# Deformable convolution on one core: strips sampled in six units of tap row and column half, instead of two column halves

## The reference, cut to what matters

```python
om = conv3x3_same(align, om_w, om_b)            # per position: 8 groups x 9 taps x (dy, dx, mask)
off, mask = om[..., :144], sigmoid(om[..., 144:])
for each of the 8 channel groups (32 channels) and the 9 taps:
    val = bilinear(coarse_up, own place + tap + off) * mask    # 0 outside the image
out = einsum('bhwkc,kcf->bhwf', val, weight) + bias            # 9 x 256 channels -> 256
return relu(out) + fine_cal
```

## Time and profile before

| | |
|---|---|
| median of 3 runs | 3745.19 us |
| the profiled execution's own time | 3750.21 us |
| its span, first to last instruction | 3748.5 us |
| TensorE busy | 3383.5 us, 90% |
| VectorE busy | 2643.4 us, 71% |
| ScalarE busy | 1636.7 us, 44% |
| GpSimd busy | 1300.2 us, 35% |
| mean granted TensorE clock | 0.956 |
| `sample_and_project` | from about 1376 us to the end |

### The profile page before, as it was taken

One profiled execution on the slowest core, in us unless ns is written; L12 is line 12 of the kernel. 1 busy time (PEld: TensorE's weight loads), 2 busy tenths in 40 slices (PEclk: granted clock), 3 DMA queues, 4 the chain that ended last, 5 costly groups with the idle time before them and its releaser, 6 DMA issues.

```text
span 3748.5 us, 103646 instructions
## 1 busy us (share of the span) xinstructions
PE 3383.5 (90%) x39276; PEld 3082.7 (82%) x39276; DVE 2643.4 (71%) x4029; ACT 1636.7 (44%) x3018; POOL 1300.2 (35%) x1358
## 2 busy tenths in 40 slices
PE   8979999999999947998888998998899898988998
PEld 7869999999999936888787887887788787877888
DVE  3446666666666548878876887886887887688882
ACT  0021211211221215656654665664666665566663
POOL 1000000000000025645645555554654655455451
PEclk9989999999999978999998999998999998999998
DMA  4232232222223221111112111112111112111110
GB/s 160 78 122 42 48 72 42 48 53 39 51 51 43 32 49 30 29 32 31 31 32 32 32 33 29 31 34 32 29 33 31 30 34 36 25 33 32 31 27 23
DMA packets 352248, 159.43 MB, mean 43 GB/s; under 512 B 228724, under 2 KB 346884, under 8 KB 351620
## 3 DMA queue, kind: packets, MB, share of 16 engines
q1 hardware_dynamic: 325456, 109.56, 17.4%
q10 hardware_dynamic: 21724, 26.37, 2.1%
q0 software_dynamic: 4608, 16.78, 1.2%
HBM read 104.60 MB, written 55.23 MB: 43 GB/s over the span
## 4 chain that ended last, share of the span: by engine, by line
PE 44%; issue 7%; ACT 6%; DVE 2%; POOL 2%; ACTq 1%; DMA 1%; SPq 1%; POOLq 0%; DVEq 0%
PE eb L1420 25%; PE tb L981 9%; PE vb L1003 9%; ACT wtT L986 4%; ACT ot L1025 1%; ACT res L1012 1%; DVE wt L975 1%; PE tb L911 1%; DMA win<-cpad 1%; ACTq L1316 1%; PE vb L1018 1%; ACT val L1289 1%; ACTq L882 0%; DVE val L1362 0%; SPq L1083 0%
## 5 line engine op out<-in xcount | busy, mean ns | idle before, releaser
L1420 PE MATMUL eb<-val,wd 128*128 128x256 f32 (+2 forms) x8172 | 1269.5, 300 | 9.5 <-POOL gate L1212 8.5
L1420 PEld LDWEIGHTS eb<-val,wd 128*128 128x128 f32 x8172 | 1080.6, 199 | 44.8 <-issue 35.4
L975 DVE TENSOR_TENSOR wt<-taps_all 128x576 f32<-128x576 f32 x1024 | 938.6, 984 | 52.5 <-PE tb L981 44.6
L981 PE MATMUL tb<-ident,wt 128*128 128x128 f32 x4608 | 715.9, 282 | 63.8 <-ACT wtT L986 45.3
L986 ACT COPY wtT<-tb 128x512 f32<-128x512 f32 x1152 | 651.8, 593 | 164.8 <-PE tb L981 126.0
L1362 DVE TENSOR_TENSOR val<-vb,val 128x432 fp32r<-128x432 f32 (+1 forms) x768 | 382.6, 552 | 411.0 <-ACT val L1289 409.2
L981 PEld LDWEIGHTS tb<-ident,wt 128*128 128x128 f32 x4608 | 504.7, 141 | 185.5 <-ACT wtT L986 103.6
L1289 ACT CAST val<-vb 128x432 fp32r<-128x432 f32 (+1 forms) x768 | 342.1, 524 | 706.4 <-PE vb L1003 706.2
L480 PE MATMUL conv<-fine,wf 128*108 128x256 f32 x4608 | 591.1, 289 | 7.6 <-DVE omT L751 7.6
L480 PEld LDWEIGHTS conv<-fine,wf 128*108 128x108 f32 x4608 | 570.5, 173 | 23.0 <-issue 23.0
L1003 PE MATMUL vb<-wtT,win 64*32 64x144 f32 x16384 | 350.2, 309 | 184.3 <-issue 93.3
(11 more groups left out here) (138 smaller groups left out, 3175.7 us busy)
## 6 DMA issues: line engine op xcount, KB each, us to landing
win<-cpad SPq DMA_DIRECT2D x304, 64.0 KB
om_s<-om_d SPq DMA_DIRECT2D x1152, 12.0 KB
chunk<-in_x SPq DMA_DIRECT2D x32, 512.0 KB, 5.9
xchunk<-in_x SPq DMA_DIRECT2D x32, 512.0 KB, 4.2
r_d<-r POOLq DMA_DIRECT2D x32, 512.0 KB, 3.2
rt<-r_d SPq DMA_DIRECT2D x63, 256.0 KB, 2.9
out<-ot ACTq DMA_DIRECT2D x63, 256.0 KB, 2.2
om_d<-omT SPq DMA_DIRECT2D x64, 216.0 KB
```

Of the source, the lines that this page charges most:

```text
L975: return nc.vector.tensor_tensor(wt[:, g * NK:(g + 1) * NK, WQ * u:WQ * (u + 1)].rearrange("p k (a b) -> p k a b", a=WIN), of_group(0).uns ...
L981: last = nc.tensor.transpose(tb[b][:, 128 * j:128 * j + 128], wt[:, 4 * i + j, :], ident[:])
L1420: done = nc.tensor.matmul(eb[fo][:, W * r0:W * r1], wd[wp][:, half, k, 128 * fo:128 * fo + 128], source[:, at:at + r1 - r0, cols], start=f ...
```

## The change

**Units.** A strip is sampled in six units, `UNITS` = 6: three tap rows `d` (in the order of `ROWS` = 2, 1, 0) times two column halves. Unit `at` has `d` = at // 2 and `hx` = at % 2. `wt` and `wtT` keep their size, and hold three units (`n_sub`), each with 3 taps x 4 groups for both channel halves. One sampling matmul (`sample`) has 3 taps x 16 positions = 48 moving columns, and there are 8 x 2 x 4 = 64 in a unit, 384 in a strip, where 128 with 144 columns were. A unit's values fill two banks (`vb[b]`, one for each channel half), in two buffers. ScalarE casts both halves in one operation of 768 elements (`keep_values`), VectorE splits in two of 384. The outer products are 12 for a strip, 128 x 768 elements each (`tap_weights_of`).

**Rows and banks.** `val` has 10 rows: even parity in 2 to 5, odd in 6 to 9, rows 0 and 1 are copies of 8 and 9. So no projection matmul is in two pieces any more. The copies are made by SyncE's queue, `duplicate_rows`, once in two strips: 4 DMAs, each 128 partitions x 6 taps x one run of 2 x 66 floats (528 bytes), after the sides of the odd strip. `open_strip` of the even strip waits for them (`duplicated`). The exchange at an image's end needs no `held`. A strip projects into one bank of its own, `eb[q]`, the output halves side by side; `turn_result` writes into the same bank, and one copy of 512 elements takes it out.

**Positions** are made on VectorE (`locate`, 10 steps and `coef`), where GpSimd had `place` and `weigh`. `cap` is in two parts, in two slots.

**The order.** A slot is one unit. TensorE has in each: batch 0, 5 projection matmuls, the sampling of the unit before, batch 1, 7 projection matmuls, batch 2, 6 projection matmuls; the projection is three units behind. Windows are loaded in 8 DMAs of 32 KB, near half and far half each when their last unit is sampled.

The core of the diff (`general`, constants and the setup left out):

```diff
-        VROWS, VCOLS = 9, W + 2
+        VROWS, VCOLS = 10, W + 2
-        vb = [[bank(f"vb{u}{i}") for i in range(2)] for u in range(2)]
+        vb = [ctx.enter_context(nc.psum_tensor(f"vb{i}", [128, CH, 512], f32)) for i in range(2)]
...
+        def sample(sub, b, window):
+            for j in range(BLK):
                 for u in range(2):
-                    for g in range(GH):
+                    for c in range(GH):
                         part = slice(WQ * u, WQ * (u + 1))
-                        weights = wtT[part, g * NK:(g + 1) * NK].rearrange("p k (y x) -> p k y x", y=4)
-                        last = nc.tensor.matmul(bank_of(u, v)[32 * g:32 * g + 32, :, :, at:at + 4],
-                                                win[part, window(j), 32 * g:32 * g + 32], weights[:, :, :, 4 * j:4 * j + 4],
+                        weights = wtT[part, PER * sub:PER * (sub + 1)].rearrange("p (k c) (y x) -> p c k y x", k=3, y=4)
+                        last = nc.tensor.matmul(values_of(b)[32 * c:32 * c + 32, u, :, :, 4 * j:4 * j + 4],
+                                                win[part, window(j), 32 * c:32 * c + 32], weights[:, c, :, :, 4 * j:4 * j + 4],
                                                 start=True, stop=True)
...
+                def duplicate_rows(s):
+                    w(sp, "sides", done)
+                    w(sp, "projected", read)      # 3 * (s - 1)
+                    for v in val:
+                        for half in range(CH):
+                            sp.dma_start(v[:, half, 0:6, 0:2].bitcast(f32), v[:, half, 0:6, 8:10].bitcast(f32)
+                                         ).then_inc(sems["duplicated"], 16)
...
+            # GpSimd
+                        for at in range(UNITS):
+                            side(*unit(t, p, at, -1))
+                            if at == 0:
+                                measure(t + 1, 1 - p, 0)
+                            if at == 1:
+                                measure(t + 1, 1 - p, 1)
+                            if at == 2:
+                                open_strip(t, p, crossing if p == 0 else None)
+                            if at == TURN_AT:
+                                add_rest(t - 1)
...
+            # ScalarE
+                def slot(t, p, at):
+                    for i in range(3):
+                        if known(t, 0, ST):
+                            w(act, "batched", batch_no(t, at, i) + 1)
+                            copy_batch("act", n_sub(at), i, bank_no(t, p, at, i)).then_inc(sems["tb_out"], 1)
+                        if i == 0:
+                            keep_values(*unit(t, p, at, -1))
+                    if at == 0:
+                        taps(t + 1, 1 - p, 0)
+                    if at == OM_AT and known(t + 2, 0, ST):
+                        keep(t + 2, batch_no(t, OM_AT, 3), bank_no(t, p, OM_AT, 3))
+                    if at == 2:
+                        taps(t + 1, 1 - p, 1)
...
+            # VectorE
+                def slot(t, p, at):
+                    products(*unit(t, p, at, 2))
+                    split_values(*unit(t, p, at, -1))
+                    if at in (1, 3):
+                        begin_cap(t + 1, 1 - p, at // 2)
+                    if at in (2, 4):
+                        end_cap(t + 1, 1 - p, at // 2 - 1)
+                    if at == 5:
+                        locate(t + 2, p)
...
+            # TensorE; OM_AT, FINISH_AT, TURN_AT, RESULT_AT = 1, 3, 4, 5
+                def project_part(s, p, d, half, piece):
+                    if known(s, 0, ST + 1):
+                        if half == 0 and piece == 0:
+                            w(pe, "ready", s + 1)
+                            if d == 0:
+                                w(pe, "ob_out", s - 1)
+                            elif known(s, 0, ST):
+                                w(pe, "sides", UNITS * s + 2 * d + 2)
+                        last = project(s, p, d, range(EACH * half + AFTER[piece], EACH * half + AFTER[piece + 1]))
+                def slot(t, p, at):
+                    target, q, pos = unit(t, p, at, -3)
+                    for i in range(3):
+                        if known(t, 0, ST):
+                            if i == 0:
+                                w(pe, "products", 2 * (n + 1))
+                            w(pe, "tb_out", batch_no(t, at, i) - 1)
+                            transpose_batch(n_sub(at), i, bank_no(t, p, at, i)).then_inc(sems["batched"], 1)
+                        project_part(target, q, pos // 2, pos % 2, i)
+                        if i == 0:
+                            sample_unit(*unit(t, p, at, -1))
+                    if at == OM_AT and known(t + 2, 0, ST):
+                        offsets_turn(t + 2, batch_no(t, OM_AT, 3), bank_no(t, p, OM_AT, 3))
+                    if at == TURN_AT and known(t - 1, 0, ST + 1):
+                        w(pe, "summed", t)
+                        turn_result(1 - p, m).then_inc(sems["turned"], 1)
```

More of the change, by code:

```diff
@@ L1048, in known, with unit @@
                 return not isinstance(v, int) or least <= v < end
+            def unit(t, p, at, ahead):
+                n = at + ahead
+                more, pos = n // UNITS, n % UNITS
+                return t + more, (p + more) % 2, pos
             def loop(e, strips):
@@ L1122, in sp_fast @@
                     load_offsets(sp, s, True, sems["om_loaded"])
-                strip(0, 0, None)
-                for i in range(1, 4):
-                    strip(0, i, i)
-                with sp.Fori(1, 4) as m:
-                    for i in range(4):
-                        strip(0, 4 * m + i, i)
+                batch(0)
                 with sp.Fori(1, B - 1) as b:
@@ L1257, in pool_fast @@
                     strips(it)
-                for it in range(8 * B - 1, 8 * B + 2):
+                for it in range(8 * B - 1, 8 * B + 1):
                     strips(it)
@@ L1413, in project @@
                         source = val[vp][:, half, k]
[L1414 to L1421 removed]
+                        first, last = d == 0 and n == 0, d == 2 and n == len(todo[d]) - 1
+                        at = dy + 4 * q
+                        done = nc.tensor.matmul(eb[q][:, 256 * fo:256 * fo + rows], wd[wp][:, half, k, 128 * fo:128 * fo + 128],
+                                                source[:, at:at + rows // W, cols], start=first, stop=last)
                     return done
@@ L1578, in dve_general @@
[L1578 to L1584 removed]
+                                        dst = sums[u][hx][:, 3 * ROWS[d]:3 * ROWS[d] + 3]
```

614 lines of the change are left out of this document (279 added, 335 removed).

## The result

The changed kernel took 4179.73 us (median of 4 runs, 4173.78 to 4195.98), the kernel before 3744.85 us (4 runs): a ratio of 1.117, 95% interval 1.113 to 1.121. It is 435 us slower, where 3910 us was forecast. The profiled execution took 4173.78 us with a span of 4172.1.

What follows compares the result with a forecast made beforehand. TensorE was taken as the bound: a strip of 30.6 us work plus 6.75 of waits is +2.35, times 64 +150; with +15 for image starts on 3750.2, less 5, 3910 us. Range 3650 to 4110.

Steps and rivals of the forecast that it cites:

- The sign: Whole kernel: slower 0.71, faster 0.24, same 0.05.
- Sampling's pace: TensorE's sampling bursts: 0.0085 us a matmul, 8.2 us a strip, +2.7 over the kernel before.
- The order's waits: TensorE waits for work GpSimd lists behind `side`: 2.4 (`measure`, slot 1), 0.8 (`ready`, slot 2), 1.85 us (`add_rest`, slot 4).
- The gate: `ready` on GpSimd, slot 2: done at 5.5 us against 5.4; with VectorE's `cap`, a wait of 0.8 us (0.1 to 1.5).
- The cast: ScalarE's cast of a unit's samples: begins 2.77 us into a slot and takes 0.8 us.
- in every second strip the 3.11 us of the loop's turn lie there instead. Together 1.7: Slot 1's first projection matmuls wait for side columns, or TensorE's loop turns there: 1.7 us a strip (1.55 to 3.4).
- Some 3.9 us are waits: Kernel before, per strip: beside 29.6 us of TensorE work and 1.55 of loop turn, some 3.9 us are waits.
- The pieces: Projection matmuls no longer cut in two: -1.8 us a strip on TensorE, all on the path.
- VectorE: Takes the positions at 3.6 us; busy 31.3 us a strip, not the bound, but little is spare.
- Duplicates: DMA row copies taken as hidden in some 12 us; rival, chance 0.10: late, about 4070, or 4325 at 25 us.
- An image's start: Window loads have less time before TensorE wants them: +5 us each, three times, +15.
- Sampling stays bound by issue: Rival, chance 0.07: sampling matmuls stay at 0.0172 us each, +6.7 us a strip, about 4340 us.

Runs made afterwards that it cites:

- e13_changed_unrolled: Changed kernel with `measure` and `add_rest` moved ahead of `side` and middle column's projection first (3879 us), TensorE's loop unrolled by seven pairs of strips: 3869 us, ratio 1.032.
- e4_before_ten_rows: The kernel before with only the changed kernel's ten-row layout of values, shared rows copied by DMA: 3665 us, ratio 0.978.
- e7_after_wide: Changed kernel with one sampling matmul of 96 columns for two of 48 (values wrong, only time of use): 3976 us, ratio 1.062.
- e9_first_and_wide: Changed kernel with `measure` and `add_rest` ahead of `side`, and 96-column sampling matmuls (values wrong): 3683 us, ratio 0.983.

## Why the prediction was wrong

The sign (slower, with a chance of 0.71) and the order of the waits on other engines were right; 3910 us was 270 too low, and the range ended at 4110. Two steps failed: the price of fetching instructions, and the 3.9 us of the kernel before that were taken for waits. TensorE's waits in the ten strips of the kernel before (all but one of 0.3 us), then the three kinds of issue gap in those of the changed kernel:

```profile
PE vb L1003 <- issue: 16.6, 5, 3.5
PE vb L1003 <- ACT wtT L986: 8.2, 5, 1.6
...
PE tb L981 <- ACT wtT L986: 5.6, 10, 0.6
...
PE tb L911 <- ACT wtT L986: 2.1, 11, 0.2
```

```profile
PE vb L1012 <- issue: 18.1, 14, 1.8
...
PE tb L993 <- issue: 15.4, 10, 2.0
...
PE eb L1462 <- issue: 2.9, 5, 0.8
```

- **Sampling's pace** was right. Forecast 128 matmuls in 1.37 us with the way in and out of the burst (0.0085 each and 0.28); a clean burst takes 1.31, a clean slot 5.01 for 4.95. The 25 ns between starts of the Trainium skill ("TensorE: Matmul & The Clock Gate", section "Wait — 56ns, not 53.3ns?"), already doubted then, do not hold for this tiling: the starts are 10.2 ns apart on average.
- **The order's waits**, 2.4, 0.8 and 1.85 us a strip, 5.05 in all: 323 us. The runs that moved `measure` and `add_rest` gave 248, with the side columns 301. In the trace the addition costs 1.57 a strip (ten strips), the copy 1.28 as a mean and 2.42 where it shows in full. The gate costs 1.54 and is the mis-sized one. Only a part of that is the side column (0.78 us for 0.49). The cast was even a little early (it begins 2.60 us into the slot for 2.77); what was late was VectorE. The forecast gave it 2.3 us of `cap` ahead of slot 2, but did not carry the late distances of slot 0 on to it.
- **"in every second strip the 3.11 us of the loop's turn lie there instead. Together 1.7"** is the step that failed. I took the one gap of the kernel before and carried it over, as a price of the jump. The changed kernel has three times the sampling instructions, and fetching them was priced at nothing more. The trace has 3.64 us of issue a strip (18.1 + 15.4 + 2.9 over ten) and 0.39 for the side columns, 4.03 for 1.7: some 149 us over 64 strips. `e13_changed_unrolled` and the packets show that these gaps are no price of the jump. All waits that the trace counts come to 8.4 us a strip for the 6.75 forecast.
- **"Some 3.9 us are waits"** failed too, and as much hangs on it. These 3.9 us are what the sum of the kernel before left over beside the loop's turn. The trace of its ten strips shows only 1.6 us a strip of such waits, and 1.7 for the turn. The other 2.1 to 2.3 us were neither work in the sum nor a wait, and the forecast dropped them when it put the new waits in by name. They are still there: work was forecast at 30.6 us a strip, and 41.88 less 8.4 leaves 33.5, 2.9 more. At 2.1 us over 64 strips that is some 134 of the 270 us.
- **The clock** is a part of that rest and was no term of the sum. By the granted clock of the ten strips, 0.96 for 0.98, it costs at most 1.7 us a strip now and 0.7 before, an estimate (0.04 x 41.88, 0.02 x 34.98). A strip of the kernel before at clock 1.00 (31.70 us) has a rest of 1.5 us with no clock in it: 27.8 by the prediction's sum without the pieces, 2.4 of waits. A part is that a gap's printed idle time is shorter than the loss from start to start, since ends are modelled. What the rest is beyond that stays open.
- **The pieces**: 1.8 us a strip was the price, and alone they gave 1.2 net (`e4_before_ten_rows`).
- **VectorE**: 28.4 us a strip for 31.3, the positions 3.1 us (2556.33 to 2559.38) for 3.6. Not the bound, as said. What I did not ask is whether moving them brings anything: it brought nothing, twice.
- **Duplicates** hidden, as forecast; that rival is out. **An image's start** was forecast 5 us dearer and is some 4 cheaper.
- **A reading**: 48 sampling matmuls "end at 2547.38" in the prediction. In the trace the last of them starts at 2547.26 and ends at 2547.55. Nothing hangs on it.
- **"Sampling stays bound by issue"** (4340, chance 0.07) came nearest among the rivals in kind, not in number (late duplicates at 4070 are nearer to 4180), and by the wrong mechanism. It priced a slower pace within a burst; what happens is that bursts at full pace run out of instructions.

The account by runs, all from medians: before 3745; ten rows of values -80; the chain through GpSimd +301; pace and fetching of narrow sampling matmuls +249 (with the order set right). Sum 4215, measured 4180. The 35 us between were not taken apart. A wait and a gap can cover each other in the changed kernel, as `e7_after_wide` and `e9_first_and_wide` show (204 us with the waits in place, 249 without), and the starts of the images are cheaper.

## What to carry to other kernels

Cutting an operation in pieces of equal work has a price per instruction that no instruction's duration shows: beside the pace, count how many instructions a stage issues per microsecond, and look at where the profile puts idle time down to issue, whether that comes at the loop's turn or in the middle of a burst, and whether it ends a fixed time after a packet of the instruction queue has landed. When stages are made shorter, a fixed chain through three engines no longer fits behind one; in a list worked in order, put first what another engine waits for (three calls moved here: 248 us). When a sum of work and waits leaves something over, do not call it waits before the trace shows them: it may come back under the new order. And try the parts of a large change alone: the ten rows of values with TensorE's loop unrolled make a kernel of 3548 us, 5.3% faster than the one before and 15% faster than the whole change.

## What the hardware showed that was not expected

- Matmuls of 48 columns on a 64x32 piece of the array start 10.2 ns apart on average in a burst, of 72 columns 11.4 ns, of 144 columns 17.2 ns.
- Instructions run dry within one burst: after 242 and after 116 matmuls (each with its weight load), for 2.17 and 1.55 us.
- TensorE goes on 1.2 to 1.7 us after the awaited 16 KB packet of instructions has landed (158 gaps of the changed kernel), at a turn of the loop 1.9 to 2.1 us (28 gaps of the kernel before).
- A turn of TensorE's loop costs 5.3 to 5.9 us in the strips read: 3.3 to 3.9 of gap, a second gap, mostly of 1.0 to 1.3 us, and a lower clock behind them (0.91 over the strip). By the runs it is less: 15 turns fewer gave 68 us, ten fewer 49.
- GpSimd's copy of 16 elements a partition took 776 ns on average, 0.21 to 1.21 us from one to the next, where 24 elements took 487 before. Why was not tried.
